# Three PSUM banks for the expansions, and the exponentials written a second time into two others

## The reference

```python
q = (feat @ Wq.T + bq).reshape(n, H, HD)       # k and v likewise
score = jnp.einsum('ehd,ehd->eh', q[edge_dst], k[edge_src])
score = jnp.clip(score / math.sqrt(HD), -10.0, 10.0)
smax = jax.ops.segment_max(score, edge_dst, num_segments=n)
ex = jnp.exp(score - smax[edge_dst])
den = jax.ops.segment_sum(ex, edge_dst, num_segments=n)
alpha = ex / den[edge_dst]
wv = jax.ops.segment_sum(alpha[:, :, None] * v[edge_src], edge_dst, num_segments=n).reshape(n, C)
y = wv @ Wp.T + bp
```

## Time and profile before

| | us |
|---|---|
| median of 3 runs | 3935.49 (3927.24 to 3941.48) |
| the profiled execution's span | 3995.8 |
| pass one in it, 155 to 1561 | 1406 |
| busy in the whole span: PE, DVE, POOL, ACT | 2303.1, 2175.4, 1960.5, 1124.8 |

### The profile page before, as it was taken

The page is one execution under the profiler, slowest core; times in us unless marked ns, Lnnn a source line. Parts: engine busy times, 40 slices in busy tenths (PEclk is TensorE's granted clock), DMA queues, the critical chain, the costliest instruction groups (busy, mean ns, idle before and its releaser), DMA issues.

```text
span 3995.8 us, 54572 instructions
## 1 busy us (share of the span) xinstructions
PE 2303.1 (58%) x11454; PEld 1677.2 (42%) x11455; DVE 2175.4 (54%) x6197; ACT 1124.8 (28%) x2699; POOL 1960.5 (49%) x1970
## 2 busy tenths in 40 slices
PE   4456666666666664878233333333334395777776
PEld 2244444444444443756122222222122294656655
DVE  5455655556555564242344444444444596677676
ACT  0144554445544553333111111111112100111111
POOL 0255555555555553121566666666656303544443
PEclk9788877788778877988666666667666656988898
DMA  4666656666666663121677777777767505666564
GB/s 141 195 179 178 182 176 180 175 180 181 177 178 176 176 177 100 50 86 47 191 215 221 212 211 214 211 214 228 210 206 216 175 0 186 205 197 204 183 208 150
DMA packets 365707, 698.62 MB, mean 175 GB/s; under 512 B 77317, under 2 KB 247039, under 8 KB 365674
## 3 DMA queue, kind: packets, MB, share of 16 engines
q0 software_dynamic: 134784, 425.63, 36.1%
q1 hardware_dynamic: 220602, 256.40, 20.6%
q10 hardware_dynamic: 10288, 16.23, 1.1%
HBM read 597.23 MB, written 100.85 MB: 175 GB/s over the span
## 4 chain that ended last, share of the span: by engine, by line
another core or an unknown queue 27%; PE 26%; DVE 24%; issue 16%; DMA 3%; DVEq 2%; SPq 1%; POOL 1%; ACT 1%; ACTq 0%; POOLq 0%
PE ps_px L900 7%; DVE sb_prod L1622 4%; DVE sb_wide L1615 4%; DVE sb_score L1468 4%; PE ps_pa L913 3%; PE ps_px L913 2%; PE ps_px L998 2%; PE ps_px L1007 2%; PE ps_pa L1058 2%; PE ps_pn L1045 2%; DVE sb_wide L1477 1%; PE ps_px L876 1%; DVE sb_parts L1814 1%; DVE sb_prod L1462 1%
## 5 line engine op out<-in xcount | busy, mean ns | idle before, releaser
L900 PE MATMUL ps_px<-sb_parts 128*128 x2430 | 468.2, 358 | 798.8 <-DVE sb_wide L1615 563.1
L900 PEld LDWEIGHTS ps_px<-sb_parts 128*128 128x128 bf16 x2430 | 268.1, 122 | 999.4 <-DVE sb_wide L1615 625.6
L779 POOL DMA_INDIRECT sb_ring<-kv_rows,sb_idx x324 | 322.5, 995 | 357.8 <-DVE sb_wide L1477 152.6
L913 PE MATMUL ps_pa<-sb_wide,sb_onehot 128*128 128x264 f32 x864 | 302.8, 483 | 317.1 <-DVE sb_wide L1477 256.2
L779 POOL DMA_INDIRECT sb_ring<-proj_rows,sb_idx x324 | 316.5, 977 | 303.8 <-issue 170.8
L779 POOL DMA_INDIRECT sb_parts<-kv_rows,sb_idx x324 | 316.0, 975 | 206.9 <-DVE sb_wide L1477 107.4
L1142 ACT ACTIVATE sb_parts<-sb_bits,sb_nn_tab 128x768 bf16<-128x768 int16 x135 | 126.3, 937 | 1016.6 <-remote 606.9
L900 PE MATMUL ps_px<-sb_parts,sb_xwm 128*128 x2430 | 397.9, 309 | 19.2 <-ACT sb_xwm L1147 14.6
L779 POOL DMA_INDIRECT sb_w<-narrow_rows,sb_idx x324 | 315.3, 973 | 163.7 <-issue 102.2
L913 PE MATMUL ps_px<-sb_wide,sb_onehot 128*128 128x264 f32 x756 | 252.9, 466 | 197.3 <-DVE sb_wide L1477 124.3
L779 POOL DMA_INDIRECT sb_w<-feat_rows,sb_idx x162 | 158.9, 981 | 416.0 <-issue 192.3
(11 more groups left out here) (256 smaller groups left out, 4473.2 us busy)
## 6 DMA issues: line engine op xcount, KB each, us to landing
sb_bits<-dst_short SPq DMA_DIRECT2D x280, 192.0 KB
x_edges<-sb_ring SPq DMA_DIRECT2D x54, 768.0 KB
sb_slots<-x_edges SPq DMA_DIRECT2D x54, 768.0 KB
x_edges<-sb_slots SPq DMA_DIRECT2D x27, 768.0 KB
sb_w<-x_edges SPq DMA_DIRECT2D x27, 768.0 KB
sb_msg<-lo_rows SPq DMA_DIRECT2D x28, 576.0 KB
kv_rows<-sb_slots ACTq DMA_DIRECT2D x25, 256.0 KB, 2.8
sb_parts<-part_rows SPq DMA_DIRECT2D x28, 193.5 KB
```

What stands on the lines that cost most here:

```text
L779: pool.indirect_dma_start(out=out[:, i, :], out_offset=None, in_=rows, in_offset=bass.IndirectOffsetOnAxis(ap=idx[:, 2 * p + i:2 * p + i + ...
L900: mm = pe.matmul(into, hots_t[L][:, 2 * p + i, :], flat(visit_parts[:, bass.ds(parity, 1), a, 0:width]), start=(a == 0), stop=(a == 2))
L913: mm = pe.matmul(into[:, 0:C + H], onehot[:, j, :], sums_in[:, 2 * (p % FLIGHT) + i, :], start=(p % EARLY == 0 and i == 0), stop=True, ski ...
```

## The change

The ring of PSUM banks for the expansions shrinks from five banks to three (px[:, 0] to px[:, 2]). The two banks that come free, px[:, 3] and px[:, 4], take a second copy of the exponentials: ACT computes them twice, first into sums_in as before, then, behind a wait, into bank 3 + p % 2. The wait is for the messages of pair p - 2, which were the last to read that bank; at p = 0 it is for those of the last pair of the visit before. The message products read the exponentials in the bank and no longer in sums_in. The bank of the late sums stays px[:, 5], now by its own name LATE.

```diff
+BANKS = 3
+LATE = 5
+        def weight(p):
+            return px[:, BANKS + p % 2, 0:2 * H].rearrange("p (j h) -> p j h", j=2)
-        late = px[:, 5, 0:C]
+        late = px[:, LATE, 0:C]
 # expand, PE
-                    into = px[:, p % FLIGHT, i * C:i * C + width] if L == 0 else px[:, 2 * (p % RING) + i, 0:width]
+                    into = px[:, p % BANKS, i * C:i * C + width] if L == 0 else px[:, 2 * (p % RING) + i, 0:width]
 # sum_pair, PE
-                into = pa if p < EARLY else px[:, FLIGHT]
+                into = pa if p < EARLY else px[:, LATE]
 # exps, ACT
                 act.wait_ge(clp1, v * PAIRS + p + 1)
                 act.wait_ge(summed, v * PAIRS + p + 1)
-                act.activation(sums_in[:, pair(p), C:C + H], score[:, p % FLIGHT], ACT.Exp, scale=SCORE_SCALE).then_inc(exp1, 1)
+                act.activation(sums_in[:, pair(p), C:C + H], score[:, p % FLIGHT], ACT.Exp, scale=SCORE_SCALE)
+                act.wait_ge(slots_free[0], v * PAIRS + max(p - 1, 0) + PAIRS)
+                act.activation(weight(p), score[:, p % FLIGHT], ACT.Exp, scale=SCORE_SCALE).then_inc(exp1, 1)
 # DVE
-            dve.sem_inc(mul1, FLIGHT)
+            dve.sem_inc(mul1, BANKS)
-                dve.tensor_tensor(prod[:, p % 3].rearrange("p (j c) -> p j c", j=2), px[:, p % FLIGHT, :].rearrange("p (j c) -> p j c", j=2),
+                dve.tensor_tensor(prod[:, p % 3].rearrange("p (j c) -> p j c", j=2), px[:, p % BANKS, :].rearrange("p (j c) -> p j c", j=2),
                                   kv_pairs[p][:, :, 0:C], ALU.mult).then_inc(mul1, 1)
 # scores, DVE
-                dve.wait_ge(mul1, v * PAIRS + p + 1 + FLIGHT)
+                dve.wait_ge(mul1, v * PAIRS + p + 1 + BANKS)
 # messages, DVE
                 dve.tensor_tensor(sums_in[:, pair(p), 0:C].rearrange("p j (h d) -> p j h d", h=H),
                                   kv_pairs[p][:, :, C:2 * C].rearrange("p j (h d) -> p j h d", h=H),
-                                  sums_in[:, pair(p), C:C + H].unsqueeze(3).broadcast_to([P, 2, H, HD]),
+                                  weight(p).unsqueeze(3).broadcast_to([P, 2, H, HD]),
                                   ALU.mult).then_inc(slots_free[0], 1)
 # finish, "acc", DVE
-                    dve.tensor_tensor(agg[:], agg[:], px[:, FLIGHT, 0:C + H], ALU.add).then_inc(nd, 1)
+                    dve.tensor_tensor(agg[:], agg[:], px[:, LATE, 0:C + H], ALU.add).then_inc(nd, 1)
```

## The result

The changed kernel takes 3965.38 us in the median of 5 runs (3947.48 to 3972.28), the kernel before beside it 3939.29 us (3927.24 to 3951.97). The ratio is 1.0071, with a 95% interval from 1.0046 to 1.0096: slower by 26 us, where I had forecast 21.5 us faster. (The ratios are those on record; they differ a little from the ratios of the two medians, here 1.0066.)

The account below looks back on a forecast made before the run. Pass one was taken as bound by POOL's sum of gathers, issue pauses and message waits. Terms -29.5 + 1 + 4 + 3 = -21.5 us took 3935.5 to 3914 us; own range 3893 to 3924, whole range 3870 to 3975.

Parts of the forecast that it names:

- A shorter gather then shortens the pass: First edge pass: POOL's gathers, issue pauses and message waits make 1380.8 of 1406 us, so POOL's time sets the pass.
- rival (a): POOL: shorter gathers only make it stop sooner, gain given back; about 3938 us; chance 0.25 together with (d).
- Part 1: POOL's gathers in pass one: no longer held up by messages with two SBUF inputs, -29.5 us, bounds 0 and 42.5.
- Part 2: DVE's 405 messages, reading PSUM and SBUF as the products do: 1 us more, bounds 0 and 11 us.
- Part 3: ScalarE's second exponentials and their wait, mostly hidden since ACT idles half the pass: 4 us more, bounds 0 and 83.
- Rival (b): ScalarE loses up to two pairs of lead to the wait, delaying PE's sums: slower, 3975 us; chance 0.21.
- Part 4: Three banks: expansions wait for earlier products, which matters only before the first visit: 3 us more, bounds 0 and 13.
- (c): Held gathers start the late signals, so a quarter of DVE's 551 us of stalls goes too: about 3800 us; chance 0.11.
- (d): The change doesn't do what it says, gathers stay at 975 to 995 ns; counted with (a), together 0.25.
- Gather means near 949 and POOL busy near 767: Sign of a right forecast in pass one: L779's three means within a few ns of 949, POOL busy about 767 us.
- PE's sums not waiting for L1161 beyond some 30 us: Sign of a right forecast: PE's waits for ScalarE's one-hots (L1161) stay within some 30 us.
- The visits' stalls on L1462 as many as now, each cycle some 0.3 us shorter: Sign of a right forecast: DVE's products (L1462) stall as often as before, each cycle some 0.3 us shorter.

Follow-up runs that it names:

- The long pause: Kernel before, with POOL setting 16 columns to zero and waiting for that ahead of each gather of pass one: ratio 1.0528.
- the ring of three: Kernel before with three expansion banks instead of five, nothing else: ratios 1.0008 and 1.0014 with prompt updates, 1.0006 with late ones.
- the pair of runs on the 3941 us core: Kernel before with only the three-bank ring, 1.0006, and the changed kernel with messages reading the exponentials in SBUF, 1.0052, each against the kernel before.
- the increments: Kernel before with eight semaphore increments of no effect added on ScalarE per pair of pass one, behind the exponential: ratio 1.0072.
- The wait alone: Kernel before with only ScalarE's wait for the messages of pair p-2 added behind the exponential: ratios 1.0000 and 0.9995, both with prompt updates.
- messages from SBUF: Changed kernel, but messages read the exponentials in SBUF as before: against the kernel before, 1.0002 with prompt updates, 1.0052 with late ones.
- The weights moved behind the one-hots: Changed kernel with the second exponential and its wait moved behind the pair's distances and one-hots on ScalarE: 1.0086 against the kernel before.
- constant weights: Kernel before with three banks and messages reading a PSUM bank nothing writes; no second exponential, no wait: ratio 1.0059.

## Why the prediction was wrong

**The step that failed** is the last sentence of what bounds the kernel: "A shorter gather then shortens the pass", from POOL's ledger of gathers, issue pauses and waits. Busy time and idle time of any engine add up to the stretch; that they do is no sign that the engine bounds it. On a core with late updates the waits for messages are ended by DVE, DVE's stalls by PE's late updates, and these don't get shorter with the gather. The 4009 us core has it in one line: gathers 25.6 us less, POOL's idle time 67.8 us more. The -29.5 us of the sum stood for the gathers; freed by themselves they cost 0.6% on that core. With the 0.5% that ScalarE's part costs on the 3941 us core this adds up to 1.1%, and the changed kernel measures 1.1% on the 4009 us core and 0.7% for the result. The two parts come from different cores, so the sum is no more than plausible.

**Reading the stalls.** That PE's completions reach the others late while gathers are in flight was right. The long pause shows it, no run of gathers at 1.25 us and no late update, and so do the 82% of late updates that arrive in a pause of POOL. But I took the release for stricter than it is. Against rival (a) I said that in rows 4 and 5 DVE starts again after POOL stops, not before; in the earlier trace rows the product of 180.25 starts while the gathers run on until 189.93. What I drew from it was wrong in sign: that a quicker run of gathers brings the release sooner. Freed gathers alone (1.0059) lose instead; and the changed kernel with gathers 1.41 us apart (1.0033) seems to lose less than at 1.25. A denser run seems to cost more than it saves. That rests on ratios from different cores, each against the kernel before beside it, and on the shares of late updates that arrive within a run; by what path the updates are held is not shown at all.

**Part 1, the size.** 29.5 us of excess gone: measured 30.8 in the profile of the result (796.46 to 765.70) and some 54 us where updates are prompt, where POOL never stops for long and more gathers are held up (162 take over 1.05 us in the ring of three there, 83 on the 3941 us core). The Trainium skill's rule (SBUF — State Buffer, section "Who interferes with whom") that a VectorE instruction with at most one SBUF input does not contend with GpSimd agrees with the traces: the longest gather into sb_parts fell from 1485 to 958 ns on the 4009 us core. On a core of the prompt kind the forecast's sign was right, and the gain 48 us and not 21.5.

**Part 2.** 1 us for the messages; they became 8 ns shorter, so -3 us. The Trainium skill's 120 against 58 cycles (VectorE: DVE Perf Modes, the section on the TRN2 errata), as an estimate 65 ns more each, is not what this case shows: 675 ns out of PSUM against 683 out of SBUF.

**Part 3.** 4 us; by the pair of runs on the 3941 us core it is 18 us, the second term that was mis-sized. My cover, "ACT idles half of the pass", is true and hides the 73 us of exponentials and the wait where updates are prompt. With late updates ScalarE's own sequencer is slow too, mostly while POOL gathers (469 of the 533 slow instructions with the increments start then), and an instruction in its stream can cost 0.7 us there, idle time or not.

Rival (b) had the time nearly right, 3975, and half of its mechanism. Its mark was 60 us of PE waiting for one-hots. The wait alone reaches it where it costs nothing (64.1 and 59.2 us). The changed kernel stays under it, 51.7 us against 22.2, and 30.0 against 19.7 on the 4009 us core. But the two kernels that isolate ScalarE's part with late updates are over it: 97.6 us against 8.9 with messages from SBUF, 168.2 with the increments. So late one-hots may well be how ScalarE's part costs its time there; a lost lead isn't needed for that, since the increments wait for nothing and cost 28 us. The weights moved behind the one-hots speak against one-hots as most of the changed kernel's loss. The increments are 3240 instructions; the change adds some 745 records to ScalarE's stream in the pass. In proportion that is 0.17%, so the wait or the exponentials have a share in the 0.5% too, which no run separates.

**Part 4.** 3 us for the prologue. It went as told, and cost nothing. In the changed kernel's timeline expansion 7 starts only at 179.46 and expansion 8 at 193.46, behind products 4 and 5:

```profile
178.71 0.69 DVE L1469 TENSOR_TENSOR sb_prod<-ps_px,sb_ring 128x512 f32<-128x512 f32 x1 [12.42 <-remote]
...
179.46 1.46 PE L905 MATMUL ps_px<-sb_parts,sb_xwm 128*128 x6 [12.38 <-issue]
...
192.71 0.69 DVE L1469 TENSOR_TENSOR sb_prod<-ps_px,sb_ring 128x512 f32<-128x512 f32 x1 [12.51 <-remote]
193.46 1.46 PE L905 MATMUL ps_px<-sb_parts,sb_xwm 128*128 x6 [12.54 <-DVE sb_prod L1469]
```

The next products, at 194.11 and 195.98, need expansions 6 and 7 and have them; the earlier trace rows has the same two stalls, with 12.45 and 13.22 us.

**The rivals.** (a), given back in POOL's waits, was half of what happened: 376.0 us of waits, just short of the 380 that I had set as its mark, and 442.1 on the 4009 us core. It missed that the balance could turn negative. (c) is out by its own mark, product waits under 400 us: 384.6 + 81.2 = 465.8, and over 500 on the 4009 us core. Its idea, that held gathers start the late signals, has the traces against it: without them the updates are as late as before. (d) is out, with means of 945 to 954 ns.

**The signs.** Gather means near 949 and POOL busy near 767: right. "PE's sums not waiting for L1161 beyond some 30 us": wrong, 51.7. "The visits' stalls on L1462 as many as now, each cycle some 0.3 us shorter": wrong, they became somewhat fewer and longer. Counted in the trace on the 4009 us core, products stall for over 1.5 us 99 times before, by 4.9 us in the mean, and 89 times after, by 6.0 us.

## What to carry to other kernels

An engine's busy time, issue gaps and waits always add up to the stretch; before a saving on it is counted, ask whether the waits in that sum would stay as they are. Where the waits of the bounding chain are ended by nothing that the profile shows, price the change against that, and expect instructions that do no work to cost time even on an engine that idles (here 0.7%, for eight increments a pair). And time a change on several cores: this one is worth 1.5% on one kind and costs 0.7 to 1.1% on the other, and neither kernel is the better one on both; nor does any version here beat the kernel before on a core with late updates.

## What the runs showed of the hardware that was not expected

- The same kernel takes 3276 to 3278 us on two cores and 3939 to 4020 us on the others, at least five. In the first kind over 99% of the recorded updates of PE's expansions come within 0.02 us, no sequencer instruction of ScalarE takes 0.7 us in pass one, and TensorE's mean granted clock in it is 0.94 to 0.97 of the 2.4 GHz level. In the other kind the mean is 0.79 to 0.82 (0.72 in the one profile of constant weights, 0.85 with the long pause): PE stands still in the stalls and is at the 1.2 GHz level behind many of them. Two groups of four equal matmuls of the kernel before, one ahead of such a stall and one behind it:

```profile
859.61 1.05 PE L913 MATMUL ps_px<-sb_wide,sb_onehot 128*128 128x264 f32 x4
...
866.43 2.12 PE L913 MATMUL ps_px<-sb_wide,sb_onehot 128*128 128x264 f32 x4 [5.11 <-ACT sb_onehot L1161]
```

- In the second kind the updates of PE are late, and instructions of ScalarE's and SyncE's sequencers take 0.7 us at times (48 to 533 of ScalarE's in pass one; 174 to 337 of SyncE's take 0.5 to 0.8 us, against 27 to 30 in the first kind). Those of VectorE do not, nor those of GpSimd but for five in one run. It comes with gathers at 1.25 and 1.41 us, and is gone at one every 1.9 us. Most late updates arrive when POOL pauses: 82% in the kernel before, 92 and 95% in the changed one. What the path is that they share, and whether a pace of 1.5 to 1.8 us would give both prompt updates and a shorter pass, stays open.
- POOL's memset of 16 columns (0.12 us) between two gathers costs nothing, since 0.30 us lie between them anyway; a wait for it makes the gap 0.96 us.
